# Attention, int8-style feed-forward and two layer norms: another order of instructions before and inside the first group of queries

## What is computed

```
qkv = x @ W_qkv + b_qkv                      # split into q, k, v, 16 heads of 64
q = layernorm(q, q_gamma, q_beta)            # over the 64 of a head
k = layernorm(k, k_gamma, k_beta)
scores = q @ k^T / 8, masked unless 0 <= row - col < 512
attn = softmax(scores) @ v
h  = layernorm(x + attn @ W_out + b_out)
xn = h * rsqrt(mean(h^2) + 1e-6)
s  = 127 / max(|xn|) over the row
xq = clip(round(xn * s), -128, 127) / s
out = layernorm(h + xq @ (w_int8 * weight_scale)^T + bias)
```

## Time and profile before

| | us |
|---|---|
| median of 3 runs | 607.18 |
| the profiled execution, its own time | 606.79 |
| its span on the slowest core (core 1) | 605.0 |
| spans of the 8 cores | 595.1 to 605.0 |
| busy: PE, DVE, ACT, POOL | 468.6, 432.2, 353.0, 393.6 |

### The profile page before, as it was taken

One profiled execution on the slowest core, in us unless ns is written; L12 is line 12 of the kernel. 1 busy time (PEld: TensorE's weight loads), 2 busy tenths in 40 slices (PEclk: granted clock), 3 DMA queues, 4 the chain that ended last, 5 costly groups with the idle time before them and its releaser, 6 DMA issues.

```text
span 605.0 us, 9828 instructions; the slowest of 8 cores (595.1 to 605.0 us)
## 1 busy us (share of the span) xinstructions
PE 468.6 (77%) x2546; PEld 203.7 (34%) x2546; DVE 432.2 (71%) x736; ACT 353.0 (58%) x517; POOL 393.6 (65%) x429
## 2 busy tenths in 40 slices
PE   0367677788789979889989888899899785778563
PEld 0112232333334434334434333344344332233221
DVE  0435787854556899887766998877668888656885
ACT  0132465666576867757767777777677677463231
POOL 3335687756486787776767877666767876456454
PEclk9969998899999999999999999999999999799788
DMA  8666821879000000442220000231110002232002
GB/s 168 150 118 118 161 71 69 129 220 168 7 1 2 1 18 18 42 111 93 71 72 0 18 20 0 20 123 69 71 36 1 18 18 20 76 116 104 2 35 104
DMA packets 22148, 40.25 MB, mean 67 GB/s; under 512 B 13648, under 2 KB 15952, under 8 KB 20304
## 3 DMA queue, kind: packets, MB, share of 16 engines
q1 hardware_dynamic: 18864, 28.63, 15.4%
q0 software_dynamic: 3232, 11.01, 12.9%
HBM read 39.11 MB, written 8.39 MB: 79 GB/s over the span
## 4 chain that ended last, share of the span: by engine, by line
PE 43%; DVE 22%; issue 16%; ACT 11%; POOL 5%; DMA 2%; DVEq 1%; ACTq 0%; SPq 0%; POOLq 0%
PE d L293 16%; PE d L329 6%; PE ov L384 5%; PE d L350 5%; PE d L339 5%; DVE qtmp L639 3%; ACT zbq L811 3%; PE sc L365 2%; DVE qa L581 2%; DMA xh<-wqk 2%; DVE stats L612 2%; POOL wqk_s L944 2%; POOL bd L985 2%; PE sc L444 2%; DVE vt L572 2%
## 5 line engine op out<-in xcount | busy, mean ns | idle before, releaser
L959 POOL TENSOR_TENSOR pT<-pT,cb_s 128x256 bf16<-128x256 bf16 x176 | 146.8, 843 | 80.4 <-ACT pT L827 80.3
L827 ACT ACTIVATE pT<-sc 128x1024 bf16<-128x1024 f32 x136 | 138.0, 1017 | 70.9 <-PE sc L365 70.2
L293 PE MATMUL d<-xT,wqk_s 128*128 128x512 bf16 x512 | 132.2, 405 | 33.8 <-ACT zbq L811 17.7
L384 PE MATMUL ov<-pT,vt 128*128 128x512 bf16 (+1 forms) x448 | 79.8, 301 | 10.8 <-DVE qa L581 9.7
L293 PEld LDWEIGHTS d<-xT,wqk_s 128*128 128x128 bf16 x512 | 47.6, 101 | 103.5 <-issue 63.0
L938 POOL TENSOR_TENSOR sqq<-zbq 128x512 bf16<-128x512 bf16 x32 | 41.2, 1286 | 53.4 <-ACT zbq L811 53.4
L329 PE MATMUL d<-wv_s,xT 128*128 128x512 bf16 x256 | 62.1, 386 | 10.2 <-ACT zbk L811 6.6
L985 POOL TENSOR_SCALAR bd<-kT,hv 128x63 bf16<-128x63 bf16 (+1 forms) x128 | 65.5, 526 | 1.5 <-DVE kT L537 1.5
L572 DVE CAST vt<-d 128x512 bf16<-128x512 f32 x32 | 22.0, 688 | 55.9 <-PE d L329 55.7
L384 PEld LDWEIGHTS ov<-pT,vt 128*128 128x128 bf16 x448 | 42.1, 98 | 54.7 <-issue 19.2
L339 PE MATMUL d<-wo_s,qa 128*128 128x512 bf16 x192 | 45.4, 379 | 17.4 <-DVE vt L572 7.0
(11 more groups left out here) (93 smaller groups left out, 724.9 us busy)
## 6 DMA issues: line engine op xcount, KB each, us to landing
xh<-wqk SPq DMA_DIRECT2D x8, 1024.0 KB, 6.2
xh<-x SPq DMA_DIRECT2D x16, 512.0 KB, 3.3
out<-xh SPq DMA_DIRECT2D x16, 512.0 KB, 2.6
xT<-xT POOLq DMA_DIRECT2D x4, 1024.0 KB, 17.5
wv_s<-wv POOLq DMA_DIRECT2D x2, 1024.0 KB, 15.8
wo_s<-wo POOLq DMA_DIRECT2D x1, 2048.0 KB, 18.9
wf_s<-w POOLq DMA_DIRECT2D x1, 2048.0 KB, 17.4
bo_s<-bo POOLq DMA_DIRECT2D x1, 256.0 KB, 5.6
```

Of the source, the lines that this page charges most:

```text
L293: m = e.matmul(d0, wqk[:, c, k, i * 128:(i + 1) * 128], xT[g % 2][:, k, :], start=(k == 0), stop=(k == 7))
L384: m = e.matmul(ov[h][:, q0 * 128:(q0 + nq) * 128], vt[:, slot, c, 64 * h:64 * h + 128], pT[k % 4][:, h * 512 + col:h * 512 + col + nq * 12 ...
L827: e.activation(out=pT[k % 4], in_=sc[k % 2], func=AF.Exp).then_inc(s_exp, 1)
L959: return e.tensor_mul(both(t, c0, c1), both(t, c0, c1), mb)
```

## The change

The loops now begin at s = 0, and what came before (steps -3 to -1) is written out for each engine in an order of its own. In it:

- Z of pairs 0, 1 and 2 goes to the four halves of the score banks `sc`, and V units 0 to 3 to `ov`, instead of `d0`. ACT evicts these four units of V instead of DVE. Pair 1's Q and K are evicted into `pT[3]`.
- SP issues the first piece of weights first, then the constants, and the second piece only when all of `xT` of group 0 has landed. POOL fills `vt` with ones before it issues `xT`, and issues `xT` in two halves.
- Piece 0 of the weights is centred by DVE alone. Each later `centre` runs one step earlier than before (`centre(s + 5)` in step s, and not `centre(s + 4)`).
- `bqk`, the bias of Q and K, is copied by ACT instead of DVE.

Inside the first group: the third product with V of step s is issued in step s + 1, after Z for Q and the shift. ACT does the denominators behind the eviction of Q instead of ahead of it. The product of the bias of V takes half a row in step 5 and half in step 6 instead of both in step 6. `bo`, `fb` and `wo` are issued in step 2 instead of 3. Steps 8 to 31 and the tail are the same.

The diff, cut to its core:

```diff
@@ helpers
 def pv_units(s, j):
-    if 0 <= s < NP:
+    if 0 <= s < 8:
+        out += [(s, i) for i in {3: [0, 1]}.get(j, [])]
+    elif s < NP:
         out += [(s, i) for i in {3: [0, 1], 4: [2]}.get(j, [])]
-    if 8 <= s - 1 < NP:
+    if 0 <= s - 1 < 8:
+        out += [(s - 1, i) for i in {0: [2]}.get(j, [])]
+    elif 8 <= s - 1 < NP:
         out += [(s - 1, i) for i in {0: [3], 1: [4]}.get(j, [])]
...
+        def z_bank(n, i):
+            return half(sc[n % 2], i) if n < 3 else d0
+        def z_buffer(n, i):
+            return zb1[i] if n == 1 else zb[i]
+        def var_bank(n):
+            return d0 if n < 3 else d1
+        def v_bank(u):
+            return ov[u % 2] if u < 4 else d0
@@ SP
-            e.dma_start(out=cv, in_=d_cv).then_inc(s_const, 16)
-            e.dma_start(out=cb, in_=d_cb).then_inc(s_const, 16)
-            e.dma_start(out=pc, in_=d_pc).then_inc(s_const, 16)
             for c in range(8):
+                if c == 1:
+                    e.dma_start(out=cv, in_=d_cv).then_inc(s_const, 16)
+                    e.dma_start(out=pc, in_=d_pc).then_inc(s_const, 16)
+                    e.dma_start(out=cb, in_=d_cb).then_inc(s_const, 16)
+                    e.wait_ge(s_xT[0], 16)
@@ PE
-            for s in range(FIRST, NP):
+            z(0, 0)
+            z(0, 1)
+            var(0, 0)
+            var(0, 1)
+            z(1, 0)
+            z(1, 1)
+            guard(0)
+            var(1, 0)
+            var(1, 1)
+            e.wait_ge(s_cr, 1)
+            shift(0)
+            z(2, 0)
+            z(2, 1)
+            v(*v_unit(0))
+            guard(1)
+            v(*v_unit(1))
+            var(2, 0)
+            var(2, 1)
+            v(*v_unit(2))
+            v(*v_unit(3))
+
+            for s in range(NP):
...
-                    if s == FOLD and j >= 3:
+                    if FOLD <= s < FOLD + 2 and j == 3:
@@ DVE
-                e.tensor_tensor(
-                    out=wqk[:, c, 0:4].rearrange("p k (s u) -> p (k s) u", u=64),
...
+                for hf in range(2 if c < ALONE else 1):
+                    r = slice(16 * hf, 16 * hf + 16)
+                    e.tensor_tensor(
+                        out=wqk[:, c, 4 * hf:4 * hf + 4].rearrange("p k (s u) -> p (k s) u", u=64),
...
+            centre(1)
+            centre(2)
+            keys(0)
+            scale_q(0)
+            queries(0)
+            guard_max(0)
+            centre(3)
+            shift_queries(0)
+            keys(1)
+            scale_q(1)
+            queries(1)
+            guard_max(1)
+            centre(4)
...
-                if s + 4 < 8:
-                    centre(s + 4)
+                if s + 5 < 8:
+                    centre(s + 5)
@@ ACT
+            z_evict(2, 0)
+            z_evict(2, 1)
+            v_evict0(*v_unit(0))
+            v_evict0(*v_unit(1))
+            ln_var(2, 0)
+            ln_var(2, 1)
+            rstd_qk(2)
+            v_evict0(*v_unit(2))
+            v_evict0(*v_unit(3))
...
                     exp_unit(s, 0)
+                if n is not None:
+                    z_evict(n, 0)
                 if 1 <= s <= 8:
                     denominators(s - 1)
-                if n is not None:
-                    z_evict(n, 0)
@@ POOL
-            e.dma_start(out=xT[0], in_=d_xT[0]).then_inc(s_xT[0], 16)
             e.memset(vt[:, :, :, 64:128], 1.0)
+            e.dma_start(out=xT[0][:, 0:4], in_=d_xT[0][:, 0:4]).then_inc(s_xT0, 16)
+            e.dma_start(out=xT[0][:, 4:8], in_=d_xT[0][:, 4:8]).then_inc(s_xT[0], 16)
...
+            square(0, 0)
+            square(0, 1)
+            centre(1)
+            e.dma_start(out=wv[:, :, 0:512], in_=d_wv[:, :, 0:512]).then_inc(s_wv[0], 16)
+            centre(2)
+            guard_keys(0)
+            square(1, 0)
+            square(1, 1)
+            centre(3)
+            e.dma_start(out=wv[:, :, 512:E], in_=d_wv[:, :, 512:E]).then_inc(s_wv[1], 16)
...
-                if s == 3:
+                if s == 2:
                     e.dma_start(out=bo, in_=d_bo).then_inc(s_rep, 16)
...
-                    if j == 4 and s + 4 < 8:
-                        centre(s + 4)
+                    if j == 4 and s + 5 < 8:
+                        centre(s + 5)
```

160 lines of the change are left out of this document (109 added, 51 removed).

## The result

The changed kernel takes 599.49 us (median of 4 runs: 597.41, 599.18, 599.81 and 635.28) where the kernel before, on the same chip, takes 607.2: ratio 0.986, 95% interval 0.984 to 0.989. The change makes the kernel 1.4% faster. The forecast was 584.0 with a range of 577 to 593, so the sign was right and the size was not: the change gains 8 us, not 23.

The account below looks back on a forecast made before the run. Transfers and PE waits bound the start, POOL's chain the steps. Savings of 11.1 (start), 11.1 (steps 0 to 4) and 0.6 (steps 5 to 7) took 605.0 to 582.2; 1.8 around it gave 584.0 us, range 577 to 593.

Parts of the forecast that it names:

- Q is evicted at +2.4 instead of +3.52: In a step without centring, Q's eviction on ACT comes at +2.4 us from the step's first scores, formerly +3.52.
- A step without centring: Steps with no weights left to centre take 10.55 us against 11.14; only 0.2 of Q's gain reaches the guard.
- the steps keep their length: Rival: steps 0 to 4 take 57.5 us, steps 5 to 7 take 39, total 589.8; chance 0.14.
- the wait of 1.16 and the fall of the clock: In steps with centring, Z no longer waits 1.16 us for POOL, nor does PE's clock fall, costing 1.6.
- steps 0 to 7 of core 5: Forecast lengths in order: 9.6, 11.45, 11.45, 10.55, 10.55, 12.35, 13.3 and 11.45 us.
- my own signs of being wrong: First scores after 60 us, step 3 over 11.1, or the part behind step 8 changed by more than 2.
- the part behind step 8: From step 8 to the end, taken as unchanged and carried over at 436.0 us.
- The split itself buys nothing: Bias product in steps 5 and 6: each half costs 1.75 us on PE and about 0.85 for a late Z.
- 37.1 for steps 5 to 7: Steps 5 to 7 together take 37.1 us against 37.72, 0.6 less, with 36 and 39 as ends.
- The start: Everything up to the first scores, which come at 55.5 us instead of 66.63, 11.1 less; bounds 50.5 and 60.
- V's weights late: Rival: first half of V's weights lands at 48, first scores at 60.5, total up to 592 us; chance 0.09.
- The thinnest margin: Second half of V's weights should land at 55 to 60 us, needed at step 0's V at 61.

Follow-up runs that it names:

- e1: The changed kernel with the steps of the kernel before put back, so only the new start stays; 601.9 us.
- e11: The changed kernel with the third product with V back in its own step and the denominators back ahead of Q's eviction; 595.5 us.
- e14: The changed kernel with one small instruction, a fill of a spare column, put ahead of POOL's program; 595.5 us.
- g2: The changed kernel with third product and denominators in their old places, value bias copied at the start, DVE's program 7 and POOL's one instruction longer; 590.9 us.
- e8: The changed kernel with only the third product with V put back in its own step; 599.2 us.
- e2: The changed kernel with only the denominators put back ahead of Q's eviction on ACT; 610.8 us.

## Why the prediction was wrong

**The step that failed first** is "Q is evicted at +2.4 instead of +3.52". I let only Z and the denominators set Q's eviction, and took DVE's normalisation of the former Q as early. It is early in steps 2 and 4, and there +2.67 and +2.48 were near. In steps 1, 5 and 8 it ends only at +3.2 to +3.4 of the step and Q's eviction follows at once: the normalising takes 1.64 and 1.79 instead of 0.68 beside POOL's centring (1) and POOL's sum with `bo` (8), and starts behind the copy of `bvr` in step 5. That copy, moved by the change to the end of step 4, stands nowhere in my sum. In step 3 the normalising ends at +4.2, behind centring, and Z itself later still, at +6.0; in steps 6 and 7 Z is late behind the bias product, as I had it. I had even written that the next Z in step 6 cost nothing "since ACT's denominators held Q's eviction until +3.52 anyway", and did not ask what else would hold it there. A step without centring was to gain 0.6; measured by undoing both, the two moves lose 0.3 a step over steps 0 to 7 (96.7 against 94.2, falls of the clock included; 96.3 against 94.3 in the two cores without a fall), and 0.6 in step 8, which the description of the change and my sum had as untouched: the denominators of pair 7 and its last product run there. The rival "the steps keep their length" said "denominators ahead of the second exponential might simply move the wait". It was the right one, with 0.14, and still too mild: 589.8.

**The centring wait.** That "the wait of 1.16 and the fall of the clock" go was wrong. POOL's wait went; V's eviction on DVE, behind the same centring, took its place with 2.05. The queue behind the moved work on DVE was what I had not followed. By size this is the larger miss on the slowest core: steps 0 to 7 of core 5 miss the forecast by +1.0, +1.2, -0.2, +3.9, +0.2, +1.2, -0.1 and 0.0, and of the 3.9 in step 3 1.7 are the fall (core 7, without it, takes 12.8). It was one of my own signs of being wrong (step 3 over 11.1), and so was the part behind step 8. Centring earlier is still the best part of the loop: with the old order steps 0 to 4 take 57.5 instead of 62.7 or e1's 62.8, 5 us.

**The bias product.** "The split itself buys nothing" was right (0.4). The 37.1 for steps 5 to 7 is 38.3 because of the order around it, 36.7 without.

**The start** came out in the mean, 55.1 against 55.5, by luck: V started 2 late (45.1 for 43), and the stretch from there to the first scores was counted 2.6 too long (12.6 for 10.0). On core 5, the one that ended last, everything that hangs on a transfer came 2 to 5 late, V's weights 5, half of the rival "V's weights late". "The thinnest margin", V's second half at step 0, held.

**The part behind step 8** was carried over as 436.0 and measured 440.9. Of the 4.9 on the slowest core, 0.6 is step 8 (16.5 for 15.9; e11 has 15.9), some 1.4 are steps 9 to 28 without the fall, 1.4 is the fall in step 21 (18.2 for the 16.8 of the cores without it), and 1.5 steps 29 to 31 and the tail. e14 shows that one record in POOL's program brings 2.7 of the 4.4 in the means back, and g2, with old order and both paddings, all of it but 0.3. Not separated are the 0.2 to 0.3 in steps 9, 12 and 28, which every kernel with the new start has: in step 9 ACT's record 315 starts 0.19 late. ACT's program is 13 records longer there; to pad ACT was not tried.

So of the 15.2 us that the profiled execution lies above the forecast, 7.3 are steps 0 to 7, 3.0 the start of core 5, and 4.9 the part that I thought out of reach.

## What to carry to other kernels

Before work is moved behind a wait, ask what else holds that wait: work ahead of an eviction that must wait for another engine anyway is free, behind it it is not. When a move is made of two parts, price them together; here undoing one part alone changed nothing (e8) or cost 11 us (e2), and undoing both gained 4. And when a step far from the edit changes length, compare it record by record with the kernel before: here a pause in another place was worth up to half of what the edit gained, and a dummy instruction is a fair test of it.
